# Shift rows issued by GpSimd itself, and fewer transfers per stack, in a two-layer attention and FFN kernel

## What is computed

```python
scores = jnp.einsum('bhqd,bhkd->bhqk', q, k) / jnp.sqrt(jnp.float32(D_K))    # block 1
attn = jax.nn.softmax(scores, axis=-1)
out = jnp.einsum('bhqk,bhkd->bhqd', attn, v)
...
scores = jnp.where(causal[None, None], scores + alibi[None], NEG_INF)         # block 3
probs = jax.nn.softmax(scores, axis=-1)
```

## Time and profile before

| | |
|---|---|
| time, median of 3 runs | 2378.68 us (2375.28 to 2379.78) |
| the profiled execution's own time | 2384.77 us |
| its span in the trace | 2383.0 us |
| mean granted TensorE clock | 0.886 of full |
| PE busy | 2071.4 us, 87% of the span |
| DVE busy | 1453.1 us, 61% |
| ACT busy | 1164.4 us, 49% |
| POOL busy | 135.2 us, 6% |
| stage B, first to last step | about 216 to 894 us |
| stage G, first to last step | about 1522 to 2165 us |

### The profile page before, as it was taken

How to read it: one execution, slowest core, us unless ns; L and a number is a source line. 1 busy time by engine, 2 the same in 40 slices (tenths; PEclk the granted TensorE clock), 3 DMA queues, 4 the chain that set the end, 5 groups by cost and what they waited for, 6 DMA issues and landing times. The chain is left out here.

```text
span 2383.0 us, 32224 instructions
## 1 busy us (share of the span) xinstructions
PE 2071.4 (87%) x12048; PEld 1210.1 (51%) x12048; DVE 1453.1 (61%) x2484; ACT 1164.4 (49%) x2431; POOL 135.2 (6%) x171
## 2 busy tenths in 40 slices
PE   7977999999999998699999957788888888898685
PEld 5763333333333336588888846443444444445564
DVE  5317999999999956544334154565555555553667
ACT  3212787877787872232222122265555555563143
POOL 0000000000000001100000000000000000000202
PEclk9996999999999999799999979587777787786888
DMA  5455242242423103420010034211110102101411
GB/s 211 164 149 65 33 59 37 42 54 32 61 35 46 24 2 106 151 86 20 16 36 1 18 117 152 55 38 32 33 37 24 46 24 46 24 3 55 154 53 71
DMA packets 101036, 143.61 MB, mean 60 GB/s; under 512 B 32100, under 2 KB 43236, under 8 KB 100864
## 3 DMA queue, kind: packets, MB, share of 16 engines
q1 hardware_dynamic: 99664, 139.37, 23.5%
q10 hardware_dynamic: 832, 1.41, 0.4%
q0 software_dynamic: 384, 0.77, 0.1%
HBM read 93.91 MB, written 47.05 MB: 59 GB/s over the span
## 5 line engine op out<-in xcount | busy, mean ns | idle before, releaser
L755 DVE TENSOR_REDUCE maxesB<-s_psB 128x1 f32<-128x1024 f32 x512 | 602.9, 1219 | 92.6 <-PE s_psB L782 82.1
L720 ACT ACTIVATE probsB<-st_psB 128x512 f32<-128x512 f32 x1024 | 528.8, 602 | 130.4 <-PE st_psB L793 130.1
L752 DVE CUSTOM_DVE_ANT_0 junkG<-s_psG,ramp 128x896 bf16<-128x896 f32 (+7 forms) x512 | 366.2, 755 | 283.1 <-PE s_psG L782 281.5
L720 ACT ACTIVATE probsG<-st_psG 128x512 f32<-128x512 f32 (+3 forms) x768 | 335.7, 494 | 248.8 <-PE st_psG L793 130.5
L782 PE MATMUL s_psB<-k_stackB,q_stackB 48*128 48x512 f32 x1024 | 409.6, 480 | 26.4 <-DMA k_stackB<-k_parts 17.4
L793 PE MATMUL st_psB<-q_stackB,k_stackB 50*128 50x512 f32 x1024 | 376.4, 451 | 32.9 <-ACT probsB L720 5.6
L782 PE MATMUL s_psG<-k_stackG,q_stackG 52*128 52x512 f32 (+3 forms) x768 | 287.5, 488 | 103.3 <-DMA q_stackG<-mpartsG 63.5
L793 PE MATMUL st_psG<-q_stackG,k_stackG 54*128 54x512 f32 (+3 forms) x768 | 317.7, 501 | 6.8 <-ACT probsG L720 3.2
L782 PEld LDWEIGHTS s_psB<-k_stackB,q_stackB 48*128 48x128 f32 x1024 | 173.4, 190 | 242.0 <-DVE maxesB L755 167.7
L826 PE MATMUL o_psB<-probsB,v_onesB 128*32 128x512 f32 x2048 | 273.6, 606 | 0.0
L782 PEld LDWEIGHTS s_psG<-k_stackG,q_stackG 52*128 52x128 f32 x768 | 152.9, 239 | 189.5 <-DMA q_stackG<-mpartsG 71.6
(11 more groups left out here) (240 smaller groups left out, 2837.4 us busy)
## 6 DMA issues: line engine op xcount, KB each, us to landing
q_stackB<-q_parts SPq DMA_DIRECT2D x186, 64.0 KB
k_stackB<-k_parts SPq DMA_DIRECT2D x93, 128.0 KB
q_stackG<-q_parts SPq DMA_DIRECT2D x186, 64.0 KB
q_parts<-partsA SPq DMA_DIRECT2D x16, 512.0 KB, 2.8
k_parts<-partsA SPq DMA_DIRECT2D x16, 512.0 KB, 2.8
q_parts<-partsF SPq DMA_DIRECT2D x16, 512.0 KB, 2.8
k_stackG<-k_parts SPq DMA_DIRECT2D x93, 64.0 KB
xA<-in_x SPq DMA_DIRECT2D x4, 1024.0 KB
```

The costliest lines, as they stand in the source:

```text
L720: act.activation(probs[:, (i % ring) * GH + h, first:HALF], st_ps[:, n % n_st, first:HALF], ACT.Exp).then_inc(st_used, 1)
L752: dve.tensor_tensor_reduce(junk[:, n % JUNK, 0:width], scores, ramp[:, SEQ - width:SEQ], 1.0, LOWEST, ALU.add, ALU.max, out).then_inc(maxe ...
L755: dve.reduce_max(out, scores, AX.X).then_inc(maxed, 1)
```

## The change

Three edits. SP no longer issues the row transfers: POOL does, in `split_max`, right after the subtraction, behind its own wait for it (`m_parts`) and for the rows of the turn before (`m_rows`). The loads of a stack are merged over the two halves of the queries: one q transfer of 128 KB where there were two of 64 KB, and one bias transfer where there were two, so a stack goes in 14 transfers in G and in 12 in B (22 and 18 before). The first stack of a stage, of which ACT issues one side, is merged in the same way. And SP's order in an iteration is now: V of the next iteration, then the stack; the waits before them are the same ones. The final wait for all rows moves from SP to POOL.

```diff
-    n_loads = 16 * SIDES * (3 * len(Q_PARTS) + (2 if causal else 0))
+    n_loads = 16 * SIDES * (2 * len(Q_PARTS) + (1 if causal else 0))
...
-                    for half in range(2):
-                        engine.dma_start(qst[dst, buf, half, :, :].bitcast(F32), qparts(a, it, u, half)).then_inc(stacks, 16)
+                    engine.dma_start(qst[dst, buf, :, :, :].bitcast(F32), qparts(a, it, u)).then_inc(stacks, 16)
                     engine.dma_start(kst[dst, buf, :, :].bitcast(F32), kparts(b, it, u)).then_inc(stacks, 16)
                 if causal:
-                    for half in range(2):
-                        engine.dma_start(qst[SIDE * u + MAIN:SIDE * u + top, buf, half, :, :].bitcast(F32),
-                                         bias_q(it, u, half)).then_inc(stacks, 16)
+                    engine.dma_start(qst[SIDE * u + MAIN:SIDE * u + top, buf, :, :, :].bitcast(F32),
+                                     bias_q(it, u)).then_inc(stacks, 16)
...
             for it in range(ITS):
-                max_rows(2 * it)
+                if it < ITS - 1:
+                    sp.wait_ge(v_set, it + 2)
+                    load_v(it + 1)
                 if it:
                     sp.wait_ge(st_made, max(exps_of[first_of[2 * it] - 1]) + 1)
                 if it < ITS - 2:
                     sp.wait_ge(stacks, n_loads * (it + 2))
                     load_stacks(sp, it + 2)
-                if it < ITS - 1:
-                    sp.wait_ge(v_set, it + 2)
-                    load_v(it + 1)
-                max_rows(2 * it + 1)
-            sp.wait_ge(m_rows, n_rows * TURNS)
...
+            def max_rows(t):
+                it, half = divmod(t, 2)
+                pool.wait_ge(m_parts, t + 1)
+                if t:
+                    pool.wait_ge(m_rows, n_rows * t)
+                for p in range(SHIFT):
+                    for u in range(SIDES):
+                        row = SIDE * u + top + p
+                        pool.dma_start(qst[row:row + 1, it % 3, half, :, :].rearrange("r h (q c) -> r (h q) c", c=P).bitcast(F32),
+                                     mparts[GS * QT * u:GS * QT * (u + 1), p, :].bitcast(F32)).then_inc(m_rows, 16)
+
             def split_max(t):
...
                                    ALU.subtract).then_inc(m_parts, 1)
+                max_rows(t)
```

More of the change, by code:

```diff
@@ L642, in load_v @@
                 sp.dma_start(vload[:, :, :, :].rearrange("p k h d -> p k (h d)"), vrows(it)).then_inc(v_in, 16)
[L644 to L653, removed]
             load_stacks(sp, 0, range(0, 1))
@@ L699, in _ @@
                     spread(it + 1)
+            pool.wait_ge(m_rows, n_rows * TURNS)
         @block.scalar
@@ L1460, in ot, with heads_q @@
                     return oT[:, bass.ds(it, 1), half, :].rearrange("p a t -> p (a t)")
-                def heads_q(c, it, u, half):
-                    v = q_parts[layer].rearrange("c i (u j d) (f t) -> c i u f d j t", u=SIDES, d=HD, f=2)
-                    return v[c, one(it), u, half].rearrange("i d j t -> (i d) j t")
+                def heads_q(c, it, u):
+                    v = q_parts[layer].rearrange("c i (u j d) (f t) -> c i u d f j t", u=SIDES, d=HD, f=2)
+                    return v[c, it, u]
                 def heads_k(c, it, u):
@@ L1473, in v_of, with bias_q @@
                     return v_rows[layer][one(it // NG if layer else it)].rearrange("i p k c -> (i p) k c")
-                def bias_q(it, u, half):
-                    return bias_copy[one(it % NG), u, :, half].rearrange("i r (j t) -> (i r) j t", j=GS)
+                def bias_q(it, u):
+                    return bias_copy[it % NG, u].rearrange("r f (j t) -> r f j t", j=GS)
                 ctx, sb, ps, sems = phase()
```

## The result

| | before | after |
|---|---|---|
| time, median of the runs of one chip job | 2382.78 us (8 runs) | 2368.32 us (8 runs) |
| lowest and highest | 2375.28 to 2392.38 | 2356.00 to 2372.83 |
| span of the profiled execution | 2383.0 | 2369.6 |
| mean granted TensorE clock | 0.886 | 0.889 |

The ratio is 0.9932, 95% interval 0.9905 to 0.9958: 14.5 us faster, a third of the 45.3 forecast. Predicted were 2333 us, with 8 chances in 10 for 2284 to 2370; the time is just inside the range, next to its upper end.

A forecast was written before the change was run, and what follows sets the result against it. VectorE was taken to pace B; in G, TensorE stalled 57.9 us for rows queued behind SyncE's stack loads. Terms -40.5 + 4.0 + 1.4 - 10.2 = -45.3 gave 2333 us, 8 chances in 10 for 2284 to 2370.

The forecast's parts named there:

- (a, b): Rows leave SyncE's queue for GpSimd's software path: 4.70 us from split to TensorE against 4.34; G's stalls gain 40.5.
- The lead of 0.59: Time before GpSimd's first row transfer, after split and semaphore: 0.59 us taken, bounds 0 and 0.59.
- (c): Stack in 14 transfers (12 in B): some 3.6 us less of SyncE's queue, gain 0; tail beside rows 0 to 0.5 a turn.
- B loses 4.0 us for a chain beyond 4.57: Stage B: 31 turns each lose 4.70 - 4.57 = 0.13 us, since VectorE's pace leaves the rows 4.57 us.
- (d): V's load moves ahead of the stack; GpSimd's copy of V must not stand before a split: 0 us.
- (e): TensorE's clock in G: three of 13 odd turns become faster ones, 10.2 us gained; bounds nothing or 60 in all.
- The turns without cover: First turn of each stage and two at G's end lose 0.36 us each, 1.4 in all.
- (1): Rival in G: the clock stays up with short stalls, 60 instead of 10 us gained, 2284; chance 0.17 with what lies between.
- (2): Rival: VectorE's work stretches GpSimd's row issues, chain 7.23 us, a loss of 86 us, 2465; chance 0.09.
- Rival (3): GpSimd's row path is longer than summed, about 5.2 us, and the clock gives nothing: 2368 us; chance 0.10.
- c: Length of the row chain from the split's start to TensorE's start; 4.70 us forecast, gain and loss balance at 5.43.

The follow-up runs named there:

- e3: Changed kernel with SyncE holding each stack load back until the odd turn's shift rows have landed; 2275.99 us, 0.9588 of the kernel before.
- e1: Changed kernel with the stacks again in 22 transfers (18 in B), rows still from GpSimd; 2356.72 us, 0.9892 of the kernel before.
- e5: e3 with the stacks again in 22 transfers instead of 14; 2291.33 us, 0.9605 of the kernel before.
- e4: Kernel before, rows still from SyncE and nothing merged, with the stack issued behind the odd turn's rows and V ahead of them; 2324.21 us, 0.9757.
- e6: e5 with each turn's four row transfers shared, two from GpSimd and two from SyncE; 2272.61 us, 0.9527 of the kernel before.

## Why the prediction came out as it did

- **The four transfers leave at once from GpSimd (a, b): right.** Split 0.44 us, first record 0.74 behind its start. The lead of 0.59 was too long: 0.29 was measured, inside the bounds 0 and 0.59. The issue is 0.508 us, below the lower bound of 0.551. Flight behind the last issue is 1.11 with nothing beside it, where 1.28 was taken. In all 3.85 us and not 4.70.
- **The rows' flight beside the stack load (c): the step that failed.** The prediction put it as "its tail can be in flight beside the rows; 0 to 0.5 us a turn, 0 taken". The runs show 2.84 us a turn in its place (6.69 - 3.85), almost six times the upper bound. The changed kernel's chain is 6.69, and 3.85 once the load is held back (e3). In the sum this is a stall of 42.3 us where 17.4 stood. A gain of 40.5 became 15.6. The mistake was in the reading of the trace before. A turn with a SyncE flight of 1.18 us beside a long stack load looked like proof that flights don't mind company. But SyncE issued its rows behind all of the load; in the changed kernel they go out before its end. In turn 7 two of its transfers and V's are still to be issued when the split begins, and one is being issued. A resource was judged from rows in which the two never met.
- **The merged loads cost no issue time (c): wrong.** A q transfer of 128 KB takes 0.56 and the k transfer after it 0.58. A load takes a mean of 8.75 us in G (10.36 in e1's 22 transfers), not 6.5. Merging also costs the rows 0.7 us of flight a turn (e1), and a slower stage start: B's first row scores come 2.8 us later than before, G's 0.5. The prediction held at most 1.4 each for that, with 0 taken. e1, the change without it, is no slower; whether it is faster the intervals don't tell.
- **B loses 4.0 us for a chain beyond 4.57: wrong.** The chain is shorter than that (3.92 us in B's first turn), the rows have time to spare, and the steady turns are 21.1 us long as before. B's 4.6 us in the profile come from its start and from the clock in its first turn (0.69, 0.82 before). That they are close to the 4.0 is luck.
- **V's load ahead of the stack (d): right.** POOL's copy of V stands behind the rows (1651.68) and holds up no split.
- **The clock (e): wrong.** Forecast were 10.2 us from three turns of the slow kind becoming average ones. The 13 odd turns sum to 345.7 us, 345.6 before, for the stalls stayed above 2.3 us. The estimate of 4.6 us for a turn at full speed held: the turn of e3 that stays up is 20.95 us, and those of before in which the clock fell took 25.5 on the shorter side.
- **Total.** The profile's span went from 2383.0 to 2369.6, -13.4 where -45.3 stood. The stall accounts for 24.9 of the missing 31.9 and the clock for 10.2. B came out 0.6 above its term. That is 35.7, so 3.8 came in smaller pieces on the other side. The turns without cover were to lose 1.4 in all; B's first and G's last gained 0.55 each, while in G's first and in turn 29 the chain grew, from 4.36 to 4.69 and from 4.34 to 5.37. Taken with their clock, G's turns 0, 1 and 28 to 31 took 4.3 us less, its other even turns 1.3 more without their stalls, and the rest of the span 0.6 more.
- **The rivals.** (1), a clock that stays up, needed the short stalls that did not come: G's clock was 0.77. Where they came, in e3, it stayed up in 10 of 15 odd turns. Of (2), GpSimd's issues stretched by VectorE, nothing is seen: the 128 issues in B, beside a VectorE busy for 593 of 680 us, have the median of G's, 508 ns, and a maximum of 563. The rule of the Trainium skill, "SBUF — State Buffer", section "Who interferes with whom", that an instruction with at most one SBUF input outside the two-port modes doesn't contend, agrees with that. With nothing in flight beside it, the path by GpSimd is 0.48 us shorter than SyncE's on this kernel (3.85 and 4.33, e5 and e4), mostly by its issues (2.00 us for four, 2.68 by SyncE). The Trainium skill, "DMA: Bandwidth & Descriptors", section "Latency and other measured facts", has hardware descriptors reach their first byte sooner, after about 0.6 us where software ones take 1. Here the rows' first packets came 1.1 us after GpSimd's first issue (e3, turn 7: issue at 1626.44, none until 1627.5, 18 until 1627.6) and 1.3 us after SyncE's (e4, turn 7: issue at 1640.67, none until 1641.9, 9 until 1642.0); the measurement decides. Rival (3), a longer path without a clock gain at 2368, hit the time to the microsecond by luck: c was 6.69 in G, and 3.92 in B's first turn, not 5.2 in both.

Three things stay open. What makes the clock fall in an odd turn of G without a stall: e6 fell in 12 turns, e3 and e5 in 5 and 7, e4, at 0.96 us in most turns, in all 15. What delays the completion of the small transfers by 0.9 us beyond their last packet beside a stack load: no run separated the DMA engines' queues from the write of the semaphore. And why one packet of the instruction queue holds up GpSimd's rows in turn 29 and not SyncE's.

## What to carry to other kernels

- Moving a small urgent transfer to another queue frees it from the issue order, not from the traffic that is in flight beside it. Ask what that will be; hold back a load that has slack until the urgent one has landed. Here one wait was worth 82 us by the ratios (0.9588 against 0.9932), five times the change itself.
- Before a flight time is taken from a trace, look whether the traffic that it will meet was in the air in that row.
- Where the clock falls in some turns and stays up in others, stalls and clock are one sum. Judge an experiment there by both, turn by turn: e5's gain of 3.6 us in the two stage starts was swallowed by 10 us of clock.

## What the runs showed of the hardware

- Four 4 KB transfers between on-chip tiles, issued by GpSimd, take 0.29 us of lead, 0.50 each, and 1.11 from the last issue to the waiting TensorE; by SyncE 0.635 each and 1.17 or 1.18 (e4). They go as 128 packets from GpSimd and as 64 from SyncE (e4, turn 29).
- Beside a stack load in flight (0.42 MB in turn 7) the same 1.11 us becomes 3.2 to 4.6 (turns 3 to 27 of the changed kernel). Beside one packet of the instruction queue it became 1.95 to 3.13 (e3, turns 29 and 27); rows issued by SyncE kept their 1.17 beside one (the kernel before, turn 29).
- A q transfer of 128 KB keeps SyncE 0.56 us where one of 64 KB takes 0.40 to 0.45, and the unchanged 64 KB k transfer behind it 0.58 where it took 0.42. A single issue took 1.90 us with a load in flight (turn 7 of the changed kernel).
- The granted clock can fall to 1.2 GHz with no stall ahead of the turn (e6, turn 5: 23.13 us of TensorE work in 24.70; 19.00 in 20.90 in turn 3, where it stays up).
